# Gathered expert rows: split into f16 halves before TensorE turns them, eight f16 blocks per tile

## The reference, cut to what matters

```python
xn = layernorm(x)                                    # x: 8 x 512 x 512, f32
attn = rope_attention(xn, Wq, Wk, Wv, Wo)            # 16 heads of 32, causal
logits = xf @ gate_w.T                               # xf: xn as 4096 rows; 8 experts
top_vals, top_idx = top_k(logits, 2)
w = softmax(top_vals)
y_all = einsum('td,eod->teo', xf, expert_w) + expert_b
out = x + attn + sum(take(y_all, top_idx) * w)
```

## Time and profile before

| | |
|---|---|
| median of 3 runs | 992.43 us (988.22 to 993.17) |
| span of the profiled execution | 993.4 us |
| PE busy | 923.7 us, 93% |
| VectorE / ScalarE / GpSimd busy | 743.1 / 435.6 / 557.3 us |
| first 12 expert matmuls start | 430.28 us |
| last expert output scaled | 649.46 us |

### The profile page before, as it was taken

One profiled execution on the slowest core, in us unless ns is written; L12 is line 12 of the kernel. 1 busy time (PEld: TensorE's weight loads), 2 busy tenths in 40 slices (PEclk: granted clock), 3 DMA queues, 4 the chain that ended last, 5 costly groups with the idle time before them and its releaser, 6 DMA issues.

```text
span 993.4 us, 18723 instructions
## 1 busy us (share of the span) xinstructions
PE 923.7 (93%) x6557; PEld 445.9 (45%) x6589; DVE 743.1 (75%) x1327; ACT 435.6 (44%) x711; POOL 557.3 (56%) x553
## 2 busy tenths in 40 slices
PE   2899889999999999979999999979999999999887
PEld 1344434444444434435555555534444444444333
DVE  7988988898789899934444444477788887888865
ACT  5367866767765433322211122124334444344432
POOL 1545575664676546643333333167877888777641
PEclk9999999999999999999999999989999999999999
DMA  6366588788785353675555555454655564555431
GB/s 241 114 216 221 153 281 304 213 305 286 220 293 217 118 203 97 234 259 180 196 173 171 177 175 179 138 202 140 196 179 178 172 193 140 165 187 177 144 108 54
DMA packets 107963, 188.63 MB, mean 190 GB/s; under 512 B 11872, under 2 KB 65248, under 8 KB 102624
## 3 DMA queue, kind: packets, MB, share of 16 engines
q1 hardware_dynamic: 97072, 152.03, 44.3%
q0 software_dynamic: 10800, 35.40, 12.5%
HBM read 117.13 MB, written 70.25 MB: 189 GB/s over the span
## 4 chain that ended last, share of the span: by engine, by line
PE 67%; DVE 15%; POOL 6%; DMA 5%; ACT 3%; issue 2%; SPq 1%; another core or an unknown queue 0%; DVEq 0%; ACTq 0%; POOLq 0%
PE psum L949 18%; PE psum L1034 10%; PE psum L1058 6%; PE psum L984 5%; PE psum L1043 5%; PE psum L997 5%; PE psum L966 5%; PE psum L1000 4%; PE psum L926 4%; DVE top L1484 3%; DMA sum_sb<-x 2%; PE psum L968 1%; POOL gT L581 1%; DVE w_att L1333 1%; POOL y_in L620 1%
## 5 line engine op out<-in xcount | busy, mean ns | idle before, releaser
L762 ACT ACTIVATE pT<-psum,factors 128x512 f32<-128x512 f32 (+1 forms) x352 | 219.6, 640 | 250.2 <-PE psum L984 239.8
L1484 DVE TENSOR_REDUCE top<-psum 128x1 f32<-128x384 f32 (+3 forms) x352 | 210.3, 634 | 21.5 <-PE psum L968 18.9
L1034 PE MATMUL psum<-xT,w_att 128*128 128x512 f16 x768 | 195.6, 380 | 6.9 <-DVE xT L1435 4.7
L949 PE MATMUL psum<-w_exp,x_gT 128*128 x852 | 196.6, 381 | 0.6 <-DVE x_gT L1440 0.6
L610 POOL DMA_INDIRECT x_g<-xn_rows,tok_of x71 | 67.3, 948 | 136.5 <-PE psum L926 135.0
L966 PE MATMUL psum<-k_stack,q_stack 96*128 96x384 f16 (+3 forms) x512 | 127.9, 303 | 16.3 <-DVE top L1484 13.7
L984 PE MATMUL psum<-q_stack,k_stack 98*128 98x256 f16 (+3 forms) x512 | 128.6, 304 | 5.8 <-ACT pT L762 4.3
L1440 DVE TENSOR_TENSOR x_gT<-psum,x_gT 128x512 f16<-128x512 f32 x71 | 49.0, 692 | 103.2 <-ACT x_gT L786 103.1
L949 PEld LDWEIGHTS psum<-w_exp,x_gT 128*128 128x128 f16 x852 | 83.7, 98 | 86.6 <-issue 2.5
L786 ACT ACTIVATE x_gT<-psum 128x512 f16<-128x512 f32 x71 | 42.3, 597 | 171.5 <-PE psum L926 171.5
L594 POOL TENSOR_SCALAR_AFFINE_SELECT pT<-pT 128x512 f32<-128x512 f32 x128 | 97.2, 769 | 19.7 <-ACT pT L762 19.6
(11 more groups left out here) (175 smaller groups left out, 1277.9 us busy)
## 6 DMA issues: line engine op xcount, KB each, us to landing
y_rows<-y_sb SPq DMA_DIRECT2D x71, 256.0 KB, 2.2
w_in<-w_all SPq DMA_DIRECT2D x12, 1024.0 KB, 11.6
q_stack<-qk_rows SPq DMA_DIRECT2D x96, 128.0 KB, 2.6
k_stack<-qk_rows SPq DMA_DIRECT2D x96, 128.0 KB, 2.6
x_in<-x SPq DMA_DIRECT2D x8, 1024.0 KB, 10.0
qk_rows<-q_hl SPq DMA_DIRECT2D x32, 256.0 KB
qk_rows<-k_hl SPq DMA_DIRECT2D x32, 256.0 KB, 2.2
xn_rows<-x_in SPq DMA_DIRECT2D x8, 1024.0 KB, 4.9
```

Source lines behind the costliest of these rows:

```text
L762: act.activation(p_of(j, h, heads), banks[BANK_T + (NT_ * n + k) % 2][:, 0:W], ACT.Exp, scale=factors[:, 0:1]).then_inc(exp_done, 1)
L949: now = pe.matmul(banks[s % 4], x_gT[s % 4][:, xp * C + c, :], w_exp[:, bass.ds(e, 1), wp, c, :].rearrange("p e d -> p (e d)"), start=n == ...
L1034: now = pe.matmul(bank, w_att[:, what, wp, c, g * P:(g + 1) * P], xT[b % 2][:, xp * C + c, :], start=at_pass == 0, stop=at_pass == 3 * C - 1)
L1484: return dve.tensor_reduce(out=top[:, h:h + heads, i], in_=banks[BANK_S + k % 2][:, 0:heads * W].rearrange("p (h t) -> p h t", h=heads), a ...
```

## The change

The f32 rows are split before they are turned. ScalarE's new `cut_high(s)` copies `x_g` to f16 (`x_cut` high), DVE's new `cut_low(s)` writes the low half, both in the natural layout in SBUF. PE turns eight f16 blocks into one PSUM bank seen as f16 (1024 columns). ScalarE's `copy_xg(s)` then copies all 1024 columns out in one instruction. `x_cut` has four buffers in the place of `v_sb[1]`, and two others for tiles 0 and 1: for tile 0 in the place of `q_hl`, for tile 1 in that of `plain_k`, which is also that of `x_g[3]`. Buffers in old places bring new waits: `cut_high(0)` waits for the store of `q_hl` of step 18, `cut_high(1)` for the last `k_hl`, gather 3 for the turn of tile 1. A gather from tile 4 on waits for `cut_low` of the tile that had the buffer, no longer for its turn. The order changes on three engines as well: `cut_high(0)` stands inside ScalarE's step 15, turn_xg(1) comes after `times_v(15, 2)` and `times_v(15, 3)`, and on DVE `cut_low(s + 4)` comes behind `scale_y(s)`, so that `cut_low(4)` is behind the wait for the bias.

```diff
...
     w_att = at("w_att", [P, NQ, 2, C, D], F16)
     q_stack = [at(f"q_stack{u}", [P, HG, S], F16) for u in range(3)]
     k_stack = [at(f"k_stack{u}", [P, HG, S], F16) for u in range(3)]
+    v_at = place[0]
     v_sb = [at(f"v_sb{u}", [P, J, D], F32) for u in range(2)]
     o_hl = [None, at("o_hl1", [P, G, 2, S], F16)]
     trig_sb = at("trig_sb", [P, 2, S], F32)
...
     y_sb = [at(f"y_sb{u}", [P, D], F32, shared1 + 4 * D * u) for u in range(4)]
     x_gT = [at(f"x_gT{u}", [P, 2 * C, P], F16, (shared0 + 8 * D if u < 2 else shared3) + 4 * D * u) for u in range(4)]
     bias_all = at("bias_all", [P, E, D], F32, shared3 + 16 * D)
+
+    x_cut = [at("x_cut_first0", [P, 2, D], F16, shared1), at("x_cut_first1", [P, 2, D], F16, shared0 + 4 * D)]
+    x_cut += [at(f"x_cut{u}", [P, 2, D], F16, v_at + 4 * J * D + 4 * D * u) for u in range(4)]
     assert shared3 + 16 * D + 4 * E * D <= place[0]
 
 
...
     def half(bank):
         return banks[bank].bitcast(F16)
 
+    def x_cut_of(s):
+        return x_cut[s if s < 2 else 2 + s % 4]
+
     def sem(name):
         return nc.alloc_semaphore(name)
 
...
     parts_done, at_low_done, at_high_done = (sem(n) for n in ("parts_done", "at_low_done", "at_high_done"))
     tok_summed, tok_done, bias_loaded = sem("tok_summed"), sem("tok_done"), sem("bias_loaded")
     gathered = [sem(f"gathered{u}") for u in range(4)]
-    xg_turned, xg_hi, xg_lo = (sem(n) for n in ("xg_turned", "xg_hi", "xg_lo"))
+    cut_hi, cut_lo, xg_turned, xg_copied = (sem(n) for n in ("cut_hi", "cut_lo", "xg_turned", "xg_copied"))
     y_done, y_scaled = sem("y_done"), sem("y_scaled")
     y_stored = [sem(f"y_stored{u}") for u in range(4)]
     qk_summed, qk_rotated, qk_roped, qk_hi, qk_lo = (sem(n) for n in ("qk_summed", "qk_rotated", "qk_roped", "qk_hi", "qk_lo"))
...
             def gather_x(s):
                 u = s % 4
                 if s >= 4:
-                    pool.wait_ge(xg_turned, s - 3)
+                    pool.wait_ge(cut_lo, s - 3)
                 elif s < 2:
                     pool.wait_ge(sum_stored[s], 16 * (EARLY // 2))
                 else:
                     pool.wait_ge(qk_lo, rope_no(2 * (N1 + 3) - 1))
+                if s == 3:
+                    pool.wait_ge(xg_turned, 2)
                 pool.indirect_dma_start(x_g[u][:], None, xn_rows, bass.IndirectOffsetOnAxis(ap=tok_of[:, s:s + 1], axis=0))\
                     .then_inc(gathered[u], 16)
 
...
                     act.wait_ge(wo_done, J * (b - 1))
                 act.activation(o_hl[b % 2][:, n % G, 0, :], o_sb[:], ACT.Copy).then_inc(o_hi, 1)
 
-            def high_xg(s):
+            def cut_high(s):
+                act.wait_ge(gathered[s % 4], 16 * (s // 4 + 1))
+                if s == 0:
+                    act.wait_ge(qk_stored[0], 16 * (N1 + 3))
+                elif s == 1:
+                    act.wait_ge(qk_lo, rope_no(2 * (N1 + 3) - 1))
+                elif s < 6:
+                    act.wait_ge(pv_done, J * N1)
+                else:
+                    act.wait_ge(xg_turned, s - 3)
+                act.activation(x_cut_of(s)[:, 0, :], x_g[s % 4][:], ACT.Copy).then_inc(cut_hi, 1)
+
+            def copy_xg(s):
                 act.wait_ge(xg_turned, s + 1)
                 if s >= 4:
                     act.wait_ge(y_done, s - 3)
...
                     act.wait_ge(qk_roped, rope_no(2 * (N1 + 2) + s))
                 else:
                     act.wait_ge(pv_done, J * N1)
-                act.activation(x_gT[s % 4][:, 0:C, :].rearrange("p c t -> p (c t)"), banks[BANK_QV + s % 4], ACT.Copy).then_inc(xg_hi, 1)
+                act.activation(x_gT[s % 4][:].rearrange("p c t -> p (c t)"), half(BANK_QV + s % 4), ACT.Copy).then_inc(xg_copied, 1)
 
             def step(n):
                 exps(n, 0)
...
                 if n - 1 in JOB_AT:
                     high_w(JOB_AT[n - 1])
                 exps(n, 7)
+                if n == N1 - 1:
+                    cut_high(0)
                 if n + 1 < N:
                     copy_c(n + 1)
                 if n + G < N:
...
             take_v(3, V_FIRST[3])
             for n in range(N1):
                 step(n)
-            high_xg(0)
-            high_xg(1)
+            copy_xg(0)
+            cut_high(1)
+            copy_xg(1)
+            cut_high(2)
             high_o(N1 - 1)
-            for s in range(2, NTILE):
-                high_xg(s)
+            cut_high(3)
+            for s in range(NTILE):
+                if s + 2 < NTILE:
+                    copy_xg(s + 2)
+                if s + 4 < NTILE:
+                    cut_high(s + 4)
             act.wait_ge(y_scaled, NTILE)
             for u in range(4):
                 act.wait_ge(y_stored[u], 16 * len(range(u, NTILE, 4)))
...
                 return now
 
             def turn_xg(s):
-                pe.wait_ge(gathered[s % 4], 16 * (s // 4 + 1))
+                pe.wait_ge(cut_lo, s + 1)
                 if s >= 4:
-                    pe.wait_ge(xg_lo, s - 3)
+                    pe.wait_ge(xg_copied, s - 3)
                 elif s == 0:
                     pe.wait_ge(v_read, N1 + G)
                 elif s == 1:
                     pe.wait_ge(sum_done, EARLY)
                 else:
                     pe.wait_ge(o_read, N1)
-                turn_tile(x_g[s % 4][:], BANK_QV + s % 4).then_inc(xg_turned, 1)
+                for k in range(2 * C):
+                    now = pe.transpose(half(BANK_QV + s % 4)[:, k * P:(k + 1) * P],
+                                       x_cut_of(s)[:, k // C, k % C * P:(k % C + 1) * P], ident16[:])
+                now.then_inc(xg_turned, 1)
 
             def expert(s):
                 e = pe.value_load(exp_of[0:1, s:s + 1], min_val=0, max_val=E - 1)
-                pe.wait_ge(xg_lo, s + 1)
+                pe.wait_ge(xg_copied, s + 1)
                 if s >= 4:
                     pe.wait_ge(y_scaled, s - 3)
                 n = 0
...
             for n in range(N1):
                 step(n)
             turn_xg(0)
-            turn_xg(1)
             times_v(N1 - 1, 2)
             times_v(N1 - 1, 3)
+            turn_xg(1)
             pe.wait_ge(exp_of_done, 1)
             for e in range(E):
                 pe.wait_ge(w_back[e], 16)
...
                 hi, lo = (xT[b][:, h * C:(h + 1) * C, j * P:(j + 1) * P] for h in range(2))
                 dve.tensor_tensor(lo, banks[x_bank(b, j)].rearrange("p (c t) -> p c t", c=C), hi, ALU.subtract).then_inc(pe_lo_done, 1)
 
-            def low_xg(s):
-                dve.wait_ge(xg_hi, s + 1)
-                hi, lo = (x_gT[s % 4][:, h * C:(h + 1) * C, :].rearrange("p c t -> p (c t)") for h in range(2))
-                dve.tensor_tensor(lo, banks[BANK_QV + s % 4], hi, ALU.subtract).then_inc(xg_lo, 1)
+            def cut_low(s):
+                dve.wait_ge(cut_hi, s + 1)
+                hi, lo = (x_cut_of(s)[:, h, :] for h in range(2))
+                dve.tensor_tensor(lo, x_g[s % 4][:], hi, ALU.subtract).then_inc(cut_lo, 1)
+
 
             def read_tokens():
                 dve.wait_ge(tok_summed, 1)
...
             own.link(dve.tensor_copy(token16[:], token_i[:]))
             for n in range(N1):
                 step(n)
-            low_xg(0)
-            low_xg(1)
+            cut_low(0)
+            cut_low(1)
             normalise_o(N1 - 1)
-            low_xg(2)
+            cut_low(2)
+            cut_low(3)
             for s in range(NTILE):
-                if s + 3 < NTILE:
-                    low_xg(s + 3)
                 if s == 0:
                     dve.wait_ge(bias_loaded, 16)
                 scale_y(s)
+                if s + 4 < NTILE:
+                    cut_low(s + 4)
             for n in range(N1, N):
                 if n == N1 + 1:
                     for u in range(4):
```

## The result

The changed kernel takes 1007.91 us (median of 4 runs, 1006.09 to 1009.6) against 992.8 us before; the ratio is 1.0154, with a 95% interval from 1.0132 to 1.0175. That is 15.1 us slower, where 11.6 were forecast, inside the range. In a second set of executions it gave 1.0138 (1.0103 to 1.0173). The profiled execution spans 1007.8 us, 14.4 more than before.

What follows compares the result with a forecast made beforehand. PE's own time was taken to bound the steady stage, small waits the part up to tile 4. Turn 4 moving from 442.02 to 453.65 gave +11.6 us, with 0 per tile: median 1004.0, 8 in 10 from 996 to 1009.5.

Steps and rivals of the forecast that it cites:

- to PE's unit 10: PE's work in step 15 behind exps 8 on ScalarE: starts at 432.0 instead of 425.42, after 7.4 us idle.
- to turn 0, at half clock: PE restarts at 1.2 GHz after idling: 1.76 us of work takes 3.4, so turn 0 starts at 435.4.
- PE per tile: Steady stage: eight f16 turns at 55 ns replace four f32 turns, 0.44 us both; bounds -0.5 to +3 us in all.
- B: Rival, PE's turns: f16 turns cheaper, even at 34 ns each; at 32 ns -13 us in all, 991; chance 0.04.
- C: Rival, PE's turns: weight loads not hidden, 8 x 98 ns, +24 us, 1028 with the stall; chance 0.05.
- The other engines: ScalarE 1.65 us a tile, with a 1.04 us copy; DVE at most 2.28; both under PE's 3.03, so no cost.
- The wait in step 15: ScalarE's cut_high(0) waits for the store of q_hl until 430.0, putting copy_c(16) 6.6 us late; the deciding term.
- my two bounds: Landing of the store of q_hl, issued at 421.17: 428.4 by the last q_stack load, 430.15 by c_rows; 430.0 taken.
- scale_y(0) came 9.07 us after the issue of the bias: DVE's wait for the bias load: 9.07 us kept from the kernel before, so issue at 443.0 gives scale_y(0) at 452.1.
- rival A: Step 15: store of q_hl lands by 424, ScalarE not held, turn 1 still late; +3.3 us, 995.7; chance 0.10.
- What is late next is the bias: Ahead of turn 4: gather 4 has landed by 451; the bias, through scale_y(0) and cut_low(4), holds turn 4 to 453.65.
- Rival D: Step 15 delays absorbed by existing waits, gather 4 still last before turn 4; 992 to 993; chance 0.07.

Runs made afterwards that it cites:

- before_wait: Kernel before, with only ScalarE's step 15 wait for the store of q_hl of step 18 added ahead of copy_c(16); ratio 1.0044.
- cut01_elsewhere: Changed kernel with x_cut of tile 0 in rden's place and of tile 1 in turned_k's, so neither the store nor turn 1 is waited for; ratio 1.0021.
- before_bias_mid: Kernel before, with SyncE's bias load no longer waiting for gather 3, but still for gather 2; ratio 1.0006.
- cut01_bias_mid: Changed kernel with x_cut of tiles 0 and 1 in other places and the bias load no longer waiting for gather 3; ratio 1.0043.
- before_bias_early: Kernel before, with SyncE's bias load waiting for neither gather 2 nor 3, only for the last product with v; ratio 1.0002.
- cut0_elsewhere: Changed kernel with x_cut of tile 0 in the place of rden, so cut_high(0) does not wait for the store of q_hl; ratio 1.0060.
- cut01_low4_gather: Changed kernel, x_cut of tiles 0 and 1 elsewhere, cut_low(4) before the bias wait, gathers 4 and 5 before low_o(15), cut_high(1) before copy_xg(0); ratio 1.0050.
- before_gather4: Kernel before, with gather 4 alone issued ahead of low_o(15); 991.65 us in a single execution.
- low4_before_bias: Changed kernel with cut_low(4) ahead of VectorE's wait for the bias; ratio 1.0126.

## Why the prediction was right, and where it fell short

The mechanism was right in its whole order. The size was short: 11.6 us against 15.1 by the medians, and against 14.4 by the two profiled executions. Taken from the two traces, from the issue of the store of q_hl to turn 4:

| step | forecast, us | measured, us |
|---|---|---|
| store issued to cut_high(0) | 8.8 | 9.44 (422.67 to 432.11) |
| to PE's unit 10 | 2.0 | 1.89 |
| to turn 0, at half clock | 3.4 | 3.25 |
| to turn 1 | 3.1 | 3.40 |
| to gather 3 | 0.7 | 1.37 |
| to the bias load | 3.8 | 3.38 |
| to scale_y(0) | 9.07 | 10.52 |
| to turn 4 | 1.55 | 1.41 |
| sum | 32.5 | 34.66 |
| less the same stretch before | 20.85 | 20.85 |
| difference | 11.6 | 13.8 |

**PE per tile** was right: 0.45 against the 0.44 forecast. The rule of 81 ns for a stream of weight load and matmul pairs (the Trainium skill, TensorE: Matmul & The Clock Gate, Back-to-back issue gap) is not borne out here: 0.45 / 8 is 56 ns. Rivals B and C fall as well; B needed 34 ns and C 98.

**The other engines** were right: 1.02 us for the copy of 1024 columns against 1.04, 0.69 us for the subtraction from SBUF, which was the lower bound.

**The wait in step 15** was right: 8.51 us of idle on ScalarE, released by the store, and the half clock behind it. Its landing at 9.4 us after the issue (8.6 to 10.7 in the three other traces that have this wait) lay close to the later of my two bounds. Two experiments show it from both sides, +4.4 us when added to the old kernel and some -8 us when taken from the new one. That the queue makes the store late, and not the store itself, is seen in the same traces: in the kernel before, the store of k_hl, of the same 256 KB, landed 3.9 us after its issue at 430.44, when what had been issued ahead of it was back, and the 8 KB of c_rows were back after 5.8 us right behind the store of q_hl, but after 1.4 us in the changed kernel (432.92 to 434.28), where the store had landed before they were issued.

The +4.4 and the -8 differ, and my expectations did not see that they must. In the old kernel the bias comes closer behind expert 0, and the old wait before turn 4 goes. In the new one turn 1, gather 3 and the bias are one chain behind it, so the full delay arrives at turn 4.

**The term that was mis-sized** is "scale_y(0) came 9.07 us after the issue of the bias": it was 10.52, 1.45 of the 2.2 us that the stretch is longer than forecast. The rest are the step from turn 1 to gather 3 (0.7 us), the store (0.6) and turn 1 (0.3), less 0.8 in the other steps. The 9.07 was taken from before as if it were a property of the transfer, and it is not:

| kernel | bias issued, against gather 4 | issue of the bias to scale_y(0), us |
|---|---|---|
| before_wait | 3.46 us ahead | 8.17 |
| cut01_elsewhere | 2.47 ahead | 8.55 |
| before_bias_mid | 2.71 ahead | 8.75 |
| before | 0.41 ahead | 9.07 |
| cut01_bias_mid | 2.42 ahead | 9.74 |
| before_bias_early | 2.96 ahead | 11.89 |
| changed kernel, two traces | 0.32 and 0.33 behind | 10.52, 10.57 |
| cut0_elsewhere | 0.40 behind | 10.81 |
| cut01_low4_gather | 3.37 behind | 11.09 |
| before_gather4 | 2.20 behind | 11.85 |

The bias was slower wherever gather 4 had been issued ahead of it, which fits that the order counts. But before_bias_early has the other order and is as slow as the slowest, and no experiment moved the order alone. So the size of the term is shown, its cause is not.

The same error is in rival A, in part: forecast +3.3 us, and cut0_elsewhere, which is that case, gave +6. In its trace turn 4 comes 3.8 us later after the issue of the store than A had it: 1.7 behind the bias, 1.5 because PE was at half clock ahead of turn 0, and 0.8 from turn 1 to gather 3. (A's terms up to turn 1 add up to 430.1 and not to 430.3, which changes nothing in this.)

**"What is late next is the bias"** was right for turn 4, but only just. The prediction had gather 4 landed by 451, 8 us after its issue; it landed 9.9 us after, at 454.94, within 0.2 us of the bias, and low4_before_bias shows what that means: with the bias out of the way, turn 4 waits for gather 4, which costs nearly as much. Rival D is out. How the last 2 us of cut01_elsewhere divide is not settled: 0.5 us are the steady stage; turn 1, still behind copy_xg(0), cut_high(1) and cut_low(1), and the moved order on DVE were not separated. The granted clock is not what is left: over the executions it was 0.990 in the mean for cut01_elsewhere and 0.989 for the kernel before.

## What to carry to other kernels

A buffer put in an old tensor's place inherits the wait for that tensor's last reader, here a store issued behind some 6 MB of loads in one queue; ask when that reader ends, not when the tensor was last computed. Choose the place of a tensor whose reader is an engine instruction long done: moving one buffer gave back 8 of 14 us. To put such a wait where nothing is queued behind it on its engine should help as well, but was not tried. Price a wait in its own surroundings, since the same wait cost 4 us in one kernel and 8 in the other. And before a wait is taken away, look how long the engine stands at the wait ahead of it: SyncE's wait for gather 3 was worth 0.5 us, because the one for c_rows came first.

## What was not expected of the hardware

- One 2048 KB load landed 7.6 to 10.7 us after its issue, in the ten traces that name its landing. The two ends are before_bias_mid and before_bias_early, which issue it 3.4 and 2.1 us behind gather 3 and both ahead of gather 4. The cause is open.
- PE's granted clock fell in one execution and not in the other over the same instructions and the same waits: in cut0_elsewhere the eight matmuls at 426.65 took 1.51 us, in cut01_elsewhere, at 426.65 as well, 0.85 us. In both PE had waited 1.02 and 0.86 us just before. The windows from 426 to 430 us give a granted clock of 0.57 and 1.00:

```profile
426.00:430.00 4.00, 3.89 (x32) 1.47 (x36) 0.00 (x0) 1.72 (x4) 3.19 (x4) 0.57 0.91 213
```

```profile
426.00:430.00 4.00, 3.68 (x60) 1.99 (x60) 0.00 (x0) 2.95 (x5) 2.99 (x4) 1.00 1.07 250
```

Ten traces have the same two waits of 1.02 and 0.86 us in step 15. Behind them the clock fell in three (before_bias_mid, cut0_elsewhere, cut01_low4_gather) and stayed at 1.00 in seven. It goes with the spread of the times: of 31 executions of the kernel before on one chip, the fastest, 988.35 us, had a mean granted clock of 0.994, and the slowest, 995.14, one of 0.984.

- With four gathers issued in a row, VectorE was released 3.6 and 4.2 us after PE's products had ended, in two kernels, and other engines that wait for PE went on within 0.1 us of it. With three in a row, in a single execution, nothing was late, but with two in a row VectorE was 2.0 and 2.1 us behind the products in two kernels. The cause stays open.
